# Centred output weights, squares on ScalarE, routing products on GpSimd and a tail in half widths, in a transformer layer with 64 experts

## The reference

```python
x = x + layernorm(attention(layernorm(x)))       # x: 2 x 1024 tokens, 128 channels
x = x + layernorm(moe(layernorm(x)))

# attention: one latent for queries and keys, shared by all heads
latent = h @ W_basis.T;  v = h @ W_v.T + b_v
att = softmax(causal(latent @ latent.T / 8));  out = (att @ v) @ W_o.T + b_o

# moe: 64 experts of 88 rows, 8 of them for each token, plus shared ones of 176 rows
scores = sigmoid(x @ gate_w.T);  choice = scores + gate_bias
# 4 of 8 groups by the sum of their two best, then the 8 best experts in these
w = 2.5 * scores[chosen] / sum(scores[chosen])
out = sum_e w[e] * (silu(x @ Wg[e].T) * (x @ Wu[e].T)) @ Wd[e].T + shared(x)
```

## Time and profile before

| | us |
|---|---|
| median of 3 runs | 516.13 (514.34 to 518.8) |
| the profiled execution | 512.98 |
| its span, first to last instruction | 511.2 |
| PE busy | 460.2 |
| POOL, DVE, ACT busy | 344.3, 342.6, 288.5 |

### The profile page before, as it was taken

One profiled execution on the slowest core, in us unless ns is written; L12 is line 12 of the kernel. 1 busy time (PEld: TensorE's weight loads), 2 busy tenths in 40 slices (PEclk: granted clock), 3 DMA queues, 4 the chain that ended last, 5 costly groups with the idle time before them and its releaser, 6 DMA issues.

```text
span 511.2 us, 7930 instructions
## 1 busy us (share of the span) xinstructions
PE 460.2 (90%) x2092; PEld 366.0 (72%) x2092; DVE 342.6 (67%) x737; ACT 288.5 (56%) x534; POOL 344.3 (67%) x338
## 2 busy tenths in 40 slices
PE   2698768598999999999999999999999999998971
PEld 1496656366677888888888888888888888886850
DVE  3464898978756666666666666666666666665794
ACT  1366788485555656555555565655555565664530
POOL 5665656565568777777777776767776777776652
PEclk9999999689999999999999999999999999999996
DMA  7000000100001010101010101000010101000011
GB/s 189 2 2 3 0 17 15 31 2 1 1 0 49 15 33 15 31 17 31 15 31 15 31 15 31 20 26 30 16 31 15 31 15 31 15 0 0 2 33 49
DMA packets 12265, 11.58 MB, mean 23 GB/s; under 512 B 1702, under 2 KB 12246, under 8 KB 12246
## 3 DMA queue, kind: packets, MB, share of 16 engines
q1 hardware_dynamic: 11094, 11.02, 7.4%
q10 hardware_dynamic: 1152, 0.33, 0.4%
HBM read 10.30 MB, written 1.05 MB: 22 GB/s over the span
## 4 chain that ended last, share of the span: by engine, by line
PE 68%; issue 10%; DVE 10%; POOL 8%; ACT 2%; DMA 1%; ACTq 0%; POOLq 0%; DVEq 0%
PE ps L1192 21%; PE ps L1194 21%; PE ps L1193 20%; POOL lat_hi L476 3%; PE ps L1144 2%; DVE x_sb L840 1%; POOL rstd L463 1%; DVE stats L788 1%; DMA bo_sb<-in_b_o 1%; DVE up_w L917 1%; POOL w_lo L484 1%; DVE x_sb L800 1%; PE ps L1082 1%; DVE hid L927 1%; PE ps L1130 1%
## 5 line engine op out<-in xcount | busy, mean ns | idle before, releaser
L476 POOL TENSOR_TENSOR lat_hi<-hid,lat_hl 128x512 fp32r<-128x512 f32 x184 | 239.8, 1305 | 109.5 <-ACT lat_hl L699 107.3
L917 DVE TENSOR_TENSOR up_w<-ps,route_w 128x512 f32<-128x512 f32 x176 | 121.5, 691 | 109.6 <-PE ps L1194 109.4
L689 ACT ACTIVATE ps<-ps 128x512 f32<-128x512 f32 x176 | 102.5, 582 | 147.9 <-PE ps L1194 147.8
L1192 PE MATMUL ps<-x_hi,w_hi 128*128 128x512 f32 x352 | 141.1, 401 | 8.2 <-DVE hid L927 5.4
L1194 PE MATMUL ps<-x_hi,w_lo 128*128 128x512 f32 x352 | 140.1, 398 | 0.0
L1193 PE MATMUL ps<-x_lo,w_hi 128*128 128x512 f32 x352 | 140.1, 398 | 0.0
L927 DVE TENSOR_TENSOR hid<-ps,up_w 128x512 f32<-128x512 f32 x176 | 121.7, 691 | 12.4 <-ACT ps L689 3.9
L699 ACT CAST lat_hl<-hid 128x512 fp32r<-128x512 f32 x184 | 112.7, 613 | 13.6 <-DVE hid L927 11.6
L1192 PEld LDWEIGHTS ps<-x_hi,w_hi 128*128 128x128 f32 x352 | 66.7, 190 | 27.0 <-issue 6.8
L1194 PEld LDWEIGHTS ps<-x_hi,w_lo 128*128 128x128 f32 x352 | 66.8, 190 | 15.8
L1193 PEld LDWEIGHTS ps<-x_lo,w_hi 128*128 128x128 f32 x352 | 66.9, 190 | 15.5
(11 more groups left out here) (131 smaller groups left out, 384.6 us busy)
## 6 DMA issues: line engine op xcount, KB each, us to landing
w_raw<-in_w_experts SPq DMA_DIRECT2D x44, 192.0 KB, 2.3
out<-x_sb SPq DMA_DIRECT2D x4, 256.0 KB, 2.3
x_sb<-in_x SPq DMA_DIRECT2D x3, 256.0 KB, 6.7
x_sb<-in_x SPq DMA_DIRECT2D x4, 64.0 KB, 2.7
sh_raw<-in_w_shared_up SPq DMA_DIRECT2D x2, 88.0 KB
sh_raw<-in_w_shared_down SPq DMA_DIRECT2D x2, 44.0 KB
wb_sb<-in_w_basis_t ACTq DMA_DIRECT2D x2, 32.0 KB, 2.1
wv_sb<-in_w_v ACTq DMA_DIRECT2D x1, 64.0 KB, 2.4
```

The source lines that it names most:

```text
L476: g.tensor_tensor(hid_lo[:, k % DEEP, :], hid[:, k % 2, :], hid_hi[:, k % DEEP, :], ALU.subtract).then_inc(s_hlo, 1)
L689: a.activation(bank, bank, ACT.Silu).then_inc(s_gated, 1)
L917: v.tensor_tensor(up_w[:, k % 2, :], ps[:, gate_bank(k) + 1, :], route_w[:, group, 512 * q:512 * q + 512], ALU.mult).then_inc(s_upw, 1)
L1192: t_.matmul(out_, hi, mhi, start=start, stop=False)
```

## The change

- **Centred output weights.** DVE takes the mean of each row of `W_o` (transposed) and of `b_o` once (`center_weights`, B in `DVE_ORDER`), before `W_v W_o` is formed. Attention's output then has mean zero: the statistics D on DVE, `att_shift` and `shift_x1` are gone.
- **Squares on ScalarE.** `keep_att` squares each tile in PSUM with a running sum (128x129, 16 of them); the last column brings the epsilon in. POOL only takes the power (`inv_sqrt_att`).
- **Values.** DVE writes them with their bias in one operation (`keep_values`); the copy by ACT and the addition on POOL are gone.
- **Routing products on POOL.** `weigh_experts` is split in four: keep (DVE), `weigh_scores` (POOL), `sum_weights` (DVE), `write_route` (POOL). A copy in the choice of groups becomes a memset of four columns.
- **The tail.** The last quad runs in two halves of 256 tokens, 8 steps of half width. The second half accumulates in bank 6 and is added to the rest by DVE. The transposes become matmuls with `center` (identity less 1/128), which take the mean out, and scaling and residual become one DVE operation. The last two tiles have a DMA each. The tail has lists of its own.
- **Loads.** Tiles 2 and 3 of x go by ACT's queue, basis and gate weights by SP's. All four lists of the prologue are new.

```diff
-            "K0 P0 V0 Q0 A00 P1 A01 Q1 A02 A03 T00 T02 T04 C00 C01 T06 A10 A11 C02 C03 T10 T11 "
+            "K0 P0 Q0 V0 P1 A00 A01 A02 Q1 T00 T02 A03 C00 T04 C01 T06 A10 C02 C03 A11 T10 T11 "
...
+        LAST = [(q, c, 0, 512) for q in range(QUADS - 1) for c in range(SETS)]
+        LAST += [(QUADS - 1, c, lo, 256) for lo in (0, 256) for c in range(SETS)]
+        UNITS = [(q, 0, 4) for q in range(QUADS - 1)] + [(QUADS - 1, lo, 2) for lo in (0, 2)]
...
+        PE_TAIL = stages(
+            "D0 Z0 D1 D2 Z1 Z2 D3 Z3 Z4 D4 Z5 D5 Z6 D6 Z7 Z8 D7 Z9 T0 Z10 D8 D9 D10 Z11 D11 "
+            "Z12 T1 Z13 Z14 D12 D13 D14 Z15 Z16 T2 Z17 D15 D16 Z18 Z19 D17 D18 D19 T3 D20 D21 "
+            "D22 T4 "
...
+            g.tensor_scalar(center[:], ident[:], 1.0 / C, None, ALU.subtract).then_inc(s_center, 1)
...
+            def inv_sqrt_att(q):
+                pool.wait_ge(s_rstd, NORMS.index(("D", q)))
+                pool.wait_ge(s_att, 2 * q + 2)
+                if q >= 2:
+                    pool.wait_ge(s_xn2, q - 1)
+                g.tensor_tensor(rstd[:, 2 + q % 2], att_var[:, q % 2], minus_half[:],
+                                ALU.pow).then_inc(s_rstd, 1)
...
+            def weigh_scores(q):
+                pool.wait_ge(s_kept, q + 1)
+                g.tensor_tensor(left[:], left[:], scores[:, q % 2], ALU.mult).then_inc(s_picked, 1)
+            def write_route(q):
+                pool.wait_ge(s_winv, q + 1)
+                if q >= 1:
+                    pool.wait_ge(s_rtp, q)
+                g.tensor_tensor(route[:], left[:].unsqueeze(2).to_broadcast([P, 4, 2, E]),
...
-                a.copy(att[:, q % 2, 2 * h:2 * h + 2, 0:C + 1],
-                       bank[:, :, 0:C + 1]).then_inc(s_att, 1)
+                for t in range(2):
+                    a.activation(squares[:, t, 0:C + 1], bank[:, t, 0:C + 1], ACT.Square,
+                                 scale=float(C) ** -0.5,
+                                 accum_out=att_var[:, q % 2, 2 * h + t:2 * h + t + 1])
+                a.copy(att[:, q % 2, 2 * h:2 * h + 2, :], bank[:, :, 0:C]).then_inc(s_att, 1)
...
+            def center_weights():
+                dve.wait_ge(s_wvl, 16 * 4)
+                rows = (wo_sb, bo_sb)
+                for n in range(2):
+                    ins = v.bn_stats(wo_stats[:, n, :], rows[n][:])
+                link(ins)
+                for n in range(2):
+                    ins = v.bn_aggr(wo_mean[:, n, :], wo_stats[:, n, :])
+                link(ins)
+                for n in range(2):
+                    ins = v.tensor_scalar(rows[n][:], rows[n][:], wo_mean[:, n, 0:1], None,
+                                          ALU.subtract)
+                ins.then_inc(s_woc, 1)
...
+                    for t in range(n):
+                        tile = 4 * q + first + t
+                        ins = v.scalar_tensor_tensor(
+                            out=x_sb[:, tile, :], in0=ps[:, unit_bank(k), P * t:P * t + P],
+                            scalar=rstd[:, 2 + k % 2, t:t + 1], in1=x1_sb[:, tile, :],
+                            op0=ALU.mult, op1=ALU.add)
```

338 lines of the change are left out of this document (180 added, 158 removed), and 36 rows, old and new, of tables (ACT_ORDER, DVE_ORDER, PE_ORDER, POOL_ORDER).

## The result

| | before | after |
|---|---|---|
| median of 4 runs (us) | 516.46 (514.34 to 518.8) | 491.48 (490.05 to 494.1) |
| profiled execution, its span | 512.98, 511.2 | 490.94, 489.1 |
| granted clock, mean | 0.977 | 0.990 |

First the page's line of busy times, then the table by stage. The stages are cut at the same steps as in the earlier trace rows: 442.70 is just ahead of the same step's `hid` (442.71) as 456.40 before is just behind it (456.36), and 482.76 is the end of the last product.

What follows compares the result with a forecast made beforehand. PE was taken to bound the kernel, so time could come only from outside the loop: -2.8 - 3.2 + 0.8 - 1.5 - 4 = -10.7 us on 512.98, 502.3 profiled, 505.4 for the median; range 499 to 511.5.

Steps and rivals of the forecast that it cites:

- The first part of the prologue: From 20 to 88 us: DVE and POOL lose work, ACT gains squares; -1.5 us, between -5 and +3.
- the start: Kernel start: centring the weights delays the transposes, the values product moves behind the latent; +0.8 us, between 0 and +2.
- the routing chain's +1.2 us a quad: Prologue: routing products on POOL, with three hand-overs, lengthen the chain by 1.2 us a quad.
- the squares: First part of the prologue: 16 squares cost ACT 5.9 to 7.7 us and delay each half quad by 0.75.
- The second part: From 88 to 134 us: PE gets half of DVE's freed 6 us, 1 from the clock; -4, between -9 and +1.
- The tail: Up to the last product: waits shrink, PE work grows, 1.5 us idle left; 44.8 to 42.0 us, -2.8.
- Behind the last product: Last product to the span's end: shorter chain for two tiles; 10.0 to 6.8 us, -3.2, bounds -2 and -4.
- the halves don't pay: Rival for the tail: 256-column matmuls bound by weight loads, 4.2 of the tail's 6.0 us go; 509.6 us, chance 0.05.
- The loop: From 134 to 456.4 us: no step edited, counted at nothing, a matmul every 0.233 us as before.
- Only the tail pays: Rival: the prologue's lists trade one wait for another, only the tail gains; 510.6 us, chance 0.16.
- The prologue runs free: Rival: DVE stops being the prologue's limit, PE stays busy, the clock does not fall; 498 us, chance 0.12.
- Slower: POOL's queue: Rival: quad 2's routing products on POOL hold up low parts, PE stops, the clock falls; 528 us, chance 0.07.

Runs made afterwards that it cites:

- old order: The changed kernel's operations put in the order of the kernel before on all four engines; 507.42 us, ratio 0.9879.
- late down: The changed kernel with the down products of the tail's first three steps behind steps 0, 1 and 2; 495.57 us, ratio 0.9616.
- full width: The changed kernel with the last quad in 4 steps of 512 tokens instead of 8 of 256; 493.65 us, ratio 0.9612.

## Why the prediction was wrong

**The first part of the prologue is the step that failed**: "I take -1.5, between -5 and +3", beside +0.8 for the start. Up to the shared expert's first `hid` it gave 7.2 us, 5.3 of PE's idle time and 1.9 of its busy time. Four things were wrong in it. First, I read PE's idle time there, 12.8 us in many small waits, as something that single edits nibble at, and priced each edit by its own instructions against the old order. The runs show that the edits are worth nothing in the old order, and 3.9 us of idle time in the new one; I had given the order no term of its own but only what U3 and X3 trade. Second, the routing chain's +1.2 us a quad: on DVE and on POOL it gave the same time, so there was slack. Third, the squares: priced at 5.9 to 7.7 us of ScalarE and 0.75 us for each half of a quad, they cost 4.2 and 0.52, and without them nothing is won. Fourth, PE's pace at the start: I took the clock of 1.00 in the earlier trace rows as it stood, so the 1.9 us of busy time had no term in the sum.

**The second part** (-4, between -9 and +1) gave 4.6 us. The size was nearly right, in part by luck: I expected DVE's freed time to become PE's and 1 us from the clock; PE's idle time fell by 1.2 us, and the busy time by 3.4 with a clock of 0.95 for 0.90. The largest piece that was measured is the statistics: with them on DVE this piece is 3.2 us longer, 2.6 of it idle time.

**The start** (+0.8, the score rows 0.8 us later): the first exponential was 0.5 us earlier. The delay of the centring was there, 1.2 us at PE's first product, and 0.9 us of it were left at the end of `lat_hl`, which takes 0.42 us where it took 1.45 beside POOL's addition to the values. What I missed is what stands behind it: PE at twice the pace, and a copy less ahead of the exponential.

**The tail** (-2.8) gave 4.8: I left 1.5 us of idle time and there were 0.54, and the centred products and the halves cost PE 1.25 us of busy time instead of 2.2. The wait for the last weights' low part went because of the early down, as forecast and shown by late down. **Behind the last product** -3.7 for -3.2; 6.34 us for the forecast's 6.8. The pitch of a 256-wide matmul is 0.117 us as taken, so "the halves don't pay" fell; they pay 1.4 us. Tail and end together were 2.5 us more than forecast.

**The loop** at nothing, 0.233 us a matmul: it is 0.231. No step there was edited, as forecast, but that edited buffers elsewhere move the loop's own was outside of the reasoning.

**The rivals.** "Only the tail pays" fell: the prologue alone, with the old tail, took 500.67 us. "The prologue runs free" came nearest (498; its own terms add up to 497.1), and its outward sign, PE busy and the clock up, is what happened. Its mechanism did not: the stretched additions are as long as before, 530 ns against 535 (the group above; single groups of four pieces 2.88 and 2.37 us), and with the routing off POOL they fell to 425 ns without a gain in time. By the Trainium skill, "SBUF — State Buffer", section "SBUF: two separate sides", a VectorE operation with two SBUF inputs and a GpSimd operation that reads SBUF shut each other out for the whole instruction. The 2.88 us agree with it, and the 1.14 of the same additions at 46.58 us, when POOL stood still; the first group, at 32.16 us, took 1.13 beside POOL's normalisation of tokens, which does not. Either way it was not where the time was. "Slower: POOL's queue" came about in its first step and not in its outcome. For quad 2 the two products are at 97.35 and 99.03 us, the second 0.95 us late for DVE's sum, and a `hid_lo` whose high part was ready at 97.74 starts only at 100.03; DVE's next `hid` waits 2.49 us for it. But PE waits at most 0.88 us at a time there, so its three steps of lead were enough:

```profile
99.03 1.04 POOL L543 TENSOR_TENSOR route<-left,winv 128x512 f32<-128x512 f32 x1 [0.95 <-DVE winv L931]
100.03 1.27 POOL L510 TENSOR_TENSOR lat_hi<-hid,lat_hl 128x512 fp32r<-128x512 f32 x1
...
101.43 0.68 DVE L1030 TENSOR_TENSOR hid<-gated,ps 88x512 f32<-88x512 f32 x1 [2.49 <-POOL lat_hi L510]
```

What is not settled: why the old order can't use the freed time. A part the traces show: up to the first shared `hid` its kernels have 0.8 to 2.1 us more idle time than before and 2.7 to 3.3 us more busy time, since the centring delays the start, PE stays slow for longer and 1.7 us of the granted clock are lost near 80 us. Further on, near 91 to 101 us, PE waits 1.6 to 3.1 us for a route and then 2.3 to 3.8 for low weights or a `hid`, as it waits 1.7 and 3.5 us in before, which fits a chain that the order sets. But apart from one pair on ScalarE no single entry of the lists was moved alone.

## What to carry over

Price a change of operations and a change of order together: here each alone gave nothing in the prologue and both gave 11.7 us, and the likely reason (argued, not shown for any one entry of the lists) is that freed time is worth something only where the next work is queued behind it. Cut stages at the same work and not at the same time, and count PE's idle time and clock apart, since in one place the waits fell and in the next mostly the clock rose. Read PE's pace from the length of one kind of row as well, since a column of the granted clock can be silent about the start. When a steady loop changes its period though nothing in it was edited, try moving its buffers before looking for a cause in the program.

## What was not expected of the hardware

- The spacing of matmuls of 512 columns at full clock depends on where their operands lie in SBUF: 0.2296, 0.2311, 0.2319 and 0.2326 us (2.0667, 2.0800, 2.0867 and 2.0933 us a step of 9), the same in each profiled kernel of a placing, with not one instruction changed between 0.2326 and 0.2311.
- Equal prologues did not always take the same time: in full width and late down the clock took 5.1 us up to 134 us where it took 3.4 in three other kernels with that prologue, and all that followed came about 1.0 us later.
- PE begins slow and becomes fast at a time that differs between kernels: weight loads took 0.33 us until 22.5 us before, until 26.5 in the old order, and 0.19 from 19.9 us in the changed kernel. In two kernels with the same instructions and other buffers this made 2.0 us.
- Each accumulating activation is followed by a read of 0.203 us on ScalarE, but the next activation starts before its end: a 129-wide square (0.280) and its read take 0.26 us of the engine together.
